# Output projections of a fused attention stage issued one step earlier, with a second PSUM bank for the turned table rows

## The reference

```
kx  = x @ w_mod(s, k).T + k_b                  # a linear layer whose weights are scaled by a style and demodulated
A   = softmax(scores of the 16 heads of each token with each other / sqrt(32))
x   = x + (A @ kx) @ w_mod(s, o).T + o_b       # block 0
x   = x + x @ (U V) + bias                     # block 1, low rank, U from the condition
x   = x + clip((x * style) @ W2.T * d + b)     # block 2
x   = x + LN(silu(cat(h, t, m, n, r, s) @ W1 + b1) @ W2 + b2)   # block 3
```

## Time and profile before

| what | value |
|---|---|
| median of 3 runs | 1014.93 us (1014.85 to 1016.52) |
| the profiled execution | 1015.03 us, its span 1013.3 us |
| TensorE busy | 980.4 us |
| VectorE, ScalarE, GpSimd busy | 662.8, 489.6, 694.9 us |
| mean granted TensorE clock | 0.992 |

### The profile page before, as it was taken

The page is one execution under the profiler, slowest core; times in us unless marked ns, Lnnn a source line. Parts: engine busy times, 40 slices in busy tenths (PEclk is TensorE's granted clock), DMA queues, the critical chain, the costliest instruction groups (busy, mean ns, idle before and its releaser), DMA issues.

```text
span 1013.3 us, 18144 instructions
## 1 busy us (share of the span) xinstructions
PE 980.4 (97%) x6566; PEld 781.8 (77%) x6566; DVE 662.8 (65%) x1213; ACT 489.6 (48%) x765; POOL 694.9 (69%) x634
## 2 busy tenths in 40 slices
PE   9988999999999899999999999999999999999995
PEld 5566777777787677788888887888888888888884
DVE  6697767689868777666556558557556665655542
ACT  2797878777767544333333334334324324333331
POOL 5556666586666448778778768768777777777861
PEclk9999999999999999999999999999999999999998
DMA  9634664464422562332332333233223224223220
GB/s 285 223 120 143 220 219 147 162 219 145 149 74 64 188 219 87 107 107 79 117 107 76 113 121 100 79 103 120 77 93 132 66 79 158 66 78 117 77 68 32
DMA packets 58269, 125.10 MB, mean 123 GB/s; under 512 B 7891, under 2 KB 12117, under 8 KB 57156
## 3 DMA queue, kind: packets, MB, share of 16 engines
q1 hardware_dynamic: 46404, 81.98, 23.9%
q0 software_dynamic: 11776, 41.95, 13.3%
HBM read 105.96 MB, written 17.95 MB: 122 GB/s over the span
## 4 chain that ended last, share of the span: by engine, by line
PE 74%; POOL 9%; issue 6%; DVE 5%; DMA 3%; ACT 2%; SPq 1%; POOLq 0%; DVEq 0%; ACTq 0%
PE ps L592 36%; PE ps_y L599 7%; PE ps_k L680 6%; PE ps_o L599 6%; PE tp L604 4%; PE ps_v L633 2%; PE ps_s L665 2%; PE ps_u L700 1%; DMA x_in<-in_x_turned 1%; PE ps_t L713 1%; PE tp L913 1%; PE ps_vt L660 1%; DMA xb<-in_x_wide 1%; POOL h L1789 1%; PE ps_z L901 1%
## 5 line engine op out<-in xcount | busy, mean ns | idle before, releaser
L1775 POOL TENSOR_TENSOR rstd<-var_eps,half 128x1 f32<-128x1 f32 x95 | 54.1, 569 | 106.5 <-DVE var_eps L1545 105.8
L1203 ACT ACTIVATE g_out<-ps 128x512 f32<-128x512 f32 x32 | 19.1, 598 | 170.2 <-PE ps L993 131.4
L1010 ACT ACTIVATE at_diag<-at 32x512 f32<-32x512 f32 x128 | 80.5, 629 | 19.1 <-DVE at L1338 17.9
L1719 POOL TENSOR_TENSOR om<-om,bc 128x512 f32<-128x512 f32 x32 | 41.3, 1291 | 68.4 <-DVE om L1310 68.3
L1706 POOL TENSOR_SCALAR xb<-xb,bias_o 128x512 f32<-128x512 f32 x32 | 52.8, 1652 | 45.2 <-DMA xb<-in_x_wide 45.1
L1551 DVE TENSOR_SCALAR shift_n<-mean_var,rstd 128x1 f32<-128x1 f32 x96 | 20.5, 214 | 96.1 <-POOL rstd L1775 93.9
L1010 ACT ACTIVATE k_diag<-kt 32x512 f32<-32x512 f32 x128 | 80.1, 626 | 1.1
L1142 ACT ACTIVATE h<-h,shift_n,rstd 128x512 f32<-128x512 f32 x32 | 26.1, 816 | 84.3 <-DVE shift_n L1551 84.3
L1531 DVE TENSOR_TENSOR t_lo<-tp,t_hi 128x512 fp32r<-128x512 f32 x64 | 43.8, 684 | 29.7 <-ACT t_hi L1138 29.7
L680 PE MATMUL ps_k<-wk_hi,xh 128*128 128x512 f32 x128 | 53.6, 419 | 0.5 <-DVE xl L1352 0.5
L592 PE MATMUL ps<-wx_high,x_hi 128*128 128x512 f32 x128 | 53.6, 419 | 0.0
(11 more groups left out here) (295 smaller groups left out, 3195.4 us busy)
## 6 DMA issues: line engine op xcount, KB each, us to landing
raw<-in_dec_w SPq DMA_DIRECT2D x30, 512.0 KB, 5.6
x_in<-in_x_turned SPq DMA_DIRECT2D x32, 256.0 KB, 5.3
xb<-in_x_wide SPq DMA_DIRECT2D x32, 256.0 KB, 4.7
x_dram<-xb SPq DMA_DIRECT2D x32, 256.0 KB, 3.7
xt<-x_dram SPq DMA_DIRECT2D x8, 1024.0 KB, 8.2
out<-o SPq DMA_DIRECT2D x32, 256.0 KB, 2.0
raw<-in_int_W SPq DMA_DIRECT2D x7, 1024.0 KB, 6.6
id_rows<-in_id_rows SPq DMA_DIRECT2D x32, 64.0 KB
```

What stands on the lines that cost most here:

```text
L1010: last = nc.scalar.activation(dst[g, :, q, :], src[g, :, :], ACT.Copy)
L1719: nc.gpsimd.tensor_tensor(om[:, :], om[:, :], bc[:, STYLE_O, t // TB, :], ALU.mult).then_inc(mix_step, 1)
L1775: nc.gpsimd.tensor_tensor(rstd[:, k:k + 1], var_eps[:, k:k + 1], half[:, :], ALU.pow).then_inc(norm_step[k], 1)
```

## The change

`O_AT` goes from 8 to 7: every output projection, its `x1_end`, the loads, the bias and the store of its residual tile happen one step earlier. The first is in step 7, the last in step T + 6. The first projection of group g now stands in step 4g + 7, in which the low part of the group's last tile is made. The turned network rows get a place of their own in `ps_x` (`ps_rows2_t`), because `ps_o` is in use from step 7; so their turn waits for `vareps_ko` (`squares_step` 8), and `ps_last` and `ps_v_t` in the same bank move one step on, to steps 8 and 10. In the order of the steps chunk 0 comes ahead of step T + 3, and chunk 1 ahead of step T + 4. The last store of SyncE is now part of step T + 7.

```
-    O_AT = 2 * G
+    O_AT = 2 * G - 1
...
+    yield "chunk", 0
     yield "attend", T + 3
-    yield "chunk", 0
+    yield "chunk", 1
     yield "attend", T + 4
     if engine == "SP":
         yield "refine", -2
     yield "split", "x"
-    yield "chunk", 1
     yield "attend", T + 5
...
+        ps_rows2_t = ps_x[:, 0:C * MLP_ROWS].rearrange("p (c r) -> p c r", c=C)
...
 SyncE, split("s"):
-                    for p in range(3):
-                        count = len(range(p, T, 3))
-                        if p == (T - 1) % 3:
-                            sp.wait_ge(x1_ready, T)
-                            sp.dma_start(x1_dram[GROUPS - 1, :, C - 1, :], xb[p][:, :]).then_inc(x1_stored[p], 16)
...
 TensorE, project_o, first projection:
-                    pe.wait_ge(table_ready, 6)
+                    pe.wait_ge(table_ready, 3)
...
 TensorE, prepare:
                 if s == 6:
                     pe.wait_ge(mlp_step, 14)
-                    pe.wait_ge(table_ready, 3)
-                    turn_rows(mlp_h2, ps_rows_t).then_inc(rows_turned, 1)
-                if s == 7:
+                    pe.wait_ge(squares_step, 8)
+                    turn_rows(mlp_h2, ps_rows2_t).then_inc(rows_turned, 1)
+                if s == 8:
+                    pe.wait_ge(table_ready, 6)
                     pe.wait_ge(small_in, 16 * 8)
                     pe.wait_ge(squares_step, 8)
...
-                if s == 9:
+                if s == 10:
                     pe.wait_ge(low_rows_in, 16 * 6)
...
 VectorE, table_rows_t:
-                    nc.vector.tensor_scalar(table_t[:, item, :, :], ps_rows_t[:, :, LOW * j:LOW * j + TABLE], wv[:, item:item + 1], None,
+                    nc.vector.tensor_scalar(table_t[:, item, :, :], (ps_rows_t, ps_rows2_t)[n][:, :, LOW * j:LOW * j + TABLE], wv[:, item:item + 1], None,
...
 VectorE, prepare (what reads ps_last and ps_v_t):
-                if s == 8:
+                if s == 9:
...
-                if s == 10:
+                if s == 11:
```

## The result

The changed kernel takes 1036.95 us (median of 4 runs, 1035.59 to 1038.76) against 1015.58 for the kernel before in the same session (4 runs, 1014.85 to 1016.52). The ratio is 1.0217, with a 95% interval of 1.0201 to 1.0233: 2.2% slower. The profiled execution of the changed kernel took 1038.76 us, with a span of 1037.0 where before had 1013.3. So the two traces stand 23.7 us apart and the two medians 21.4; the trace of the changed kernel is of the slowest of its four runs.

What follows compares the result with a forecast made beforehand. TensorE, busy 980.4 of 1013.3 us, was taken as the bound. Loop 11.8, start 4.0 and end 3.9 us made 19.7, so 1034.6; 3.3 for one fall of the clock gave 1038, range 1027 to 1045.

Steps and rivals of the forecast that it cites:

- likeliest case: Whole kernel: the forecast itself, with one fall of the clock or none, 1032 to 1042 us, chance 0.65.
- five usual groups: Steps 11, 15, 19, 27 and 31: each group's first projection waits for `ol`, 5 x 1.73 = 8.65 us.
- step 23, wait: Step 23: projection 3.91 us late because VectorE is behind, less the 0.81 us wait already there: 3.1 us.
- step 23, clock: Behind the wait in step 23: 6.7 us at half speed lose 3.3 us, added once.
- start, steps 6 to 9: Turn waits for `vareps_ko`, step 7 gets a projection, a 1.92 us wait goes: 4.0 us late after step 9.
- end, to the turn: Steps 34 to 39: chunk 0 waits for `z`, a projection more, the second waits for `xb`: 3.9 us.
- rival (b): The loop absorbs the new waits and only the two ends are paid: 1023 us, chance 0.14.
- (c): Not slower: `ol` is ready when TensorE comes, and 2.72 and 1.92 us are gained: 1010 us, chance 0.04.
- upper bound for the loop: Loop's terms if all is paid and step 23 keeps its 0.81 us wait: 12.6 us.
- rival (a): The clock falls at the long waits in steps 6 and 34 too: 1044.6 us, chance 0.15.
- argument against a fall there: Steps 6 and 34: waits only slightly longer than the punished 2.2 us, and TensorE is dense around them.
- The gain: Mix of step 9: the 1.92 us wait at 98.19 goes, since the first residual tile is asked for earlier.

Runs made afterwards that it cites:

- e3_fill_23: Changed kernel with 14 unread matmuls in step 23 ahead of the wait for `ol`: 1036.17 us, ratio 1.0197.
- e4_old_order: Changed kernel with the old order of the chunks at the end: 1035.08 us, ratio 1.0184.
- e7_fill_6: Changed kernel with 5 unread matmuls in step 6 ahead of the wait for `vareps_ko`: 1036.42 us, ratio 1.0209.
- e2_low_first: Changed kernel with `low_o` ahead of `kb` in VectorE's order of each step: 1030.14 us, ratio 1.0137.
- e11_low_late: Changed kernel with one more unread VectorE instruction ahead of the low part of the fourth tile in groups 0 to 6: 1045.61 us, ratio 1.0312.
- e6_short_sum: Changed kernel with VectorE's addition over raw weights in step 22 cut from 2048 to 128 columns: 1033.63 us, ratio 1.0195.
- e12_order_only: Kernel before, eight steps, with only the new order of the chunks at the end: 1019.91 us, ratio 1.0056.
- e1_bank_only: Kernel before with only the turned rows in `ps_x` behind `vareps_ko`, and `ps_last` and `ps_v_t` one step later: 1015.91 us, ratio 1.0010.
- e8_all_mended: Changed kernel, seven steps kept, with `low_o` ahead of `kb`, old chunk order, and network rows turned in step 7: 1025.57 us, ratio 1.0106.
- e5_before_low_first: Kernel before, eight steps, with `low_o` ahead of `kb` on VectorE: 1014.01 us, ratio 0.9999.
- e9_fill_all: Changed kernel with unread matmuls filling step 6, step 23 and two pauses at the start of block 3: 1034.96 us, ratio 1.0200.

## Why the prediction was right

The likeliest case was the one that came: 1038.0 foretold, 1036.95 measured, inside 1027 to 1045 and inside the 1032 to 1042 of that case. The mechanism of each large wait is the one foretold. That the sum agrees to a tenth is in part luck. Its terms against the traces:

| step of the working | foretold | in the trace |
|---|---|---|
| five usual groups | 8.65 | 8.2 |
| step 23, wait | 3.1 | 2.9 (`e3_fill_23`) |
| step 23, clock | 3.3 | 2.9 (1.6 in `e4_old_order` and `e7_fill_6`) |
| start, steps 6 to 9 | 4.0 | 5.3 |
| end, to the turn | 3.9 | 3.8 |
| sum | 23.0 | 23.1 |

The start is 1.3 us over its term, by a fall of the clock that the forecast didn't count, and the other four are together 1.2 under theirs. With the fall behind step 23 at 1.6 us, as in two of the other traces, the sum would have been 21.8. The time of 1038 lies between the median of 1036.95 and the traced 1038.76.

- **The usual wait** is shown: present in seven groups, a pause of 1.38 us by which the projection is 1.54 late (1.62 foretold) and a restart of some 0.11, gone when `low_o` goes ahead of `kb` (`e2_low_first`), longer when it is made later (`e11_low_late`), and never absorbed. That settles rival (b). It also settles (c): `ol` isn't ready when TensorE comes.
- **Step 23** was right in its cause (`e6_short_sum`), and its parts come out at 2.9 and 2.9 us in the traced execution. By the prediction's own terms its upper bound for the loop is 12.7 (8.65 + 3.91 + 0.11) and not 12.6, which changes nothing.
- **The clock** is where the forecast and rival (a) each had a part. It fell in step 6, which (a) said and the forecast did not, and it did not fall in step 34 of the changed kernel. The price in step 6 was 1.6 us and not 3.3 (3.1 less 1.5, `e7_fill_6`), since it lasted some 3 us only. The prediction's argument against a fall there, that TensorE is dense around the wait, was a misreading of the earlier trace rows: they show the wait of 1.25 us at 75.69 directly ahead of the turn at 76.16, and in the changed kernel the two pauses leave TensorE 0.73 us of work in 4.00. The prediction also took how late a matmul starts for the length of the pause; the pauses are 2.32 for 2.46 in step 6, 3.62 for 3.9 in step 23 and 2.40 for 2.7 in step 34.
- **The start** was sized at 4.0 and measured 5.3. The working itself holds: without the lower clock of step 6 it is 3.7 by step 9 (`e7_fill_6`). The missing 1.6 is the clock.
- **The end** came out as worked out, with 2.40 us for `z` (2.7 foretold), 0.94 for `xb` (1.05 to 1.1) and the wait for `y` at 0.64 (0.9 foretold). `e12_order_only` adds what the prediction didn't ask: this loss comes with the order of the chunks, and needs no projection moved.
- **The gain** of the wait at the mix of step 9 was real: it is gone from TensorE's timeline, and the s7 and s9 columns grow by 2.2 only, though a whole projection (2.72) and its wait (1.5) lie between them. That the earlier load is what removed it isn't shown: in `e1_bank_only` the load is at its old time and TensorE's lateness alone did it.

Left open: how often a given pause lowers the clock, since only one execution of each kernel has a trace; and what makes up the spread of the runs of one kernel. The amount of clock lost is not the whole of it: in the session with the median of 1014.70 six runs of the kernel before have the same mean clock of 0.990 and take from 1012.49 to 1015.68 us. Where in the kernel a fall lies may count as much, and a mean doesn't show that. The traces stand 23.7 us apart and the medians 21.4, so the sum agrees with the one to 0.7 and with the other to 1.6 us.

## What to carry to other kernels

Before an operation is moved earlier, look up on which engine its last input is made and what stands ahead of it in that engine's queue: a distance of one step is worth nothing if the input is made behind an instruction that waits for the same step's products. If the bounding engine has no idle time, each wait that the move makes is paid in full and once per group, and a long one may be paid again as a lower clock behind it. A spot where another engine is late for a reason of its own (here one addition in step 22) costs about three times the usual one (4.5 to 5.8 us against 1.7), so look for the worst step and not for the mean one.

## What the runs showed of the hardware

- TensorE's clock after a pause. In the changed kernel none of the six pauses of 1.38 us was followed by a lower clock. The 1.41 in step 35 was in `e8_all_mended` (0.64) and was not in `e4_old_order`. Of the six pauses of 1.98 us in `e11_low_late` one was (step 11). The 1.9 ahead of the k products of step 5 was in `e2_low_first` and `e8_all_mended` and not in `e5_before_low_first`, and the 1.9 of the earlier trace rows was not. The 2.40 ahead of chunk 0 was in 3 traces of 8, the 2.6 ahead of the first `ps_z` of block 3 in 6 of 9, the 2.3 of step 6 in all 6 that had it, but there another pause of 1.25 us stands directly ahead. A pause of 3.05 us or more was followed by it in all 7 cases. So the same pause in the same place had both outcomes, from 1.41 to 2.6 us. The Trainium skill, "TensorE: Matmul & The Clock Gate", section "What's actually happening", says that the monitor behind the clock runs freely, out of step with the kernel, so that how many matmuls at a kernel's start are slow varies from run to run; it says so of the rise of the clock, and the 2.40 us pause, with both outcomes, shows the like for its fall.
- The clock also falls with no pause ahead of it. In step 28, 14 traces show TensorE listed as busy all along, and in 8 of them the clock goes down. Windows of the changed kernel there:

```profile
312.00:314.00 2.00, 2.00 (x18) 1.97 (x17) 0.08 (x1) 1.58 (x3) 0.00 (x0) 1.00 0.52 195
314.00:316.00 2.00, 2.00 (x34) 1.72 (x37) 0.31 (x3) 0.60 (x1) 1.53 (x1) 0.64 0.53 200
316.00:318.00 2.00, 2.00 (x44) 1.69 (x36) 1.33 (x2) 0.00 (x0) 2.00 (x3) 0.50 0.03 8
```

  Busy 2.00 of 2.00 us in each, and yet 0.64 and 0.50. What stands ahead is a row of small products into `ps_x`, 8 at a time and 2 columns wide. TensorE in the kernel before, where the same fall lies near 297 us:

```profile
294.42 0.95 PE L650 MATMUL ps_x<-pick,u_row 128*128 128x2 f32 x8
295.31 1.05 PE L854 MATMUL ps_x<-last_u,v_rows 32*128 32x2 f32 x8
296.28 1.13 PE L856 MATMUL ps_x<-last_m,r_rows 64*128 64x2 f32 x8
```

  So an engine that the profile calls busy can still lose its clock. That the small products are the cause is likely and not shown: no run changes them, and in 6 traces the same row is followed by full clock. I had not read this off the trace of before.
- What it costs. The fall behind step 23 cost 2.9 us (5.8 against 2.9 with the pause filled) where 6.10 us ran at 0.50. The Trainium skill, "TensorE: Matmul & The Clock Gate", section "HAM oscillation — how this bites in real kernels", counts half of the time at low clock as lost. By that the estimate for this fall is 3.05, and the measured 2.9 is near it. In `e4_old_order` and `e7_fill_6` the same place cost 1.6, because the clock was back sooner.
- Matmuls that nobody reads, put in front of a wait, keep the clock up: 14 in step 23, 5 in step 6 (1.08 and 1.06 us for scores and mix in place of 1.73 and 1.95). What that is worth in time is small: the medians with one place filled are 0.8 and 0.5 us lower, within the spread.
- The last product of the kernel takes 3.04 us in before and in `e9_fill_all`, and 4.62 in the changed kernel, whose clock is 0.51 in the window from 1025 to 1028 us. That moves the time by 0.15% and says nothing of the change.
